# q projected from the raw activations, its mean taken out by a one-row matmul

## What is computed

```
x = x + 0.5 * ffn(layernorm(x))
x = x + attn(layernorm(x))
x = x + 0.5 * ffn(layernorm(x))

ffn(y):  xk = mu_k*y + (1-mu_k)*y_prev ; xr = mu_r*y + (1-mu_r)*y_prev
         sigmoid(xr @ Wr.T) * (square(relu(xk @ Wk.T)) @ Wv.T)
attn(y): q, k, v = y @ Wq.T, y @ Wk.T, y @ Wv.T ; a = sigmoid(y @ Wg.T)   (16 heads of 64)
         h_t = a_t * h_(t-1) + k_t v_t^T ; out_t = q_t^T h_t
         layernorm(out) @ Wo.T
```

## Time and profile before

| | |
|---|---|
| median of 2 runs | 5537.23 us (5469.79 and 5604.68) |
| profiled execution | 5486.97 us |
| its span, slowest core (core 0) | 5485.4 us |
| spans of the eight cores | 5455.2 to 5485.4 us |
| mean granted TensorE clock, core 0 | 0.750 |
| TensorE matmul busy | 4035.2 us, 74% |
| DVE busy | 2755.5 us, 50% |
| ACT busy | 1614.2 us, 29% |
| POOL busy | 705.8 us, 13% |

### The profile page before, as it was taken

How to read it: one execution, slowest core, us unless ns; L and a number is a source line. 1 busy time by engine, 2 the same in 40 slices (tenths; PEclk the granted TensorE clock), 3 DMA queues, 4 the chain that set the end, 5 groups by cost and what they waited for, 6 DMA issues and landing times.

```text
span 5485.4 us, 74827 instructions; the slowest of 8 cores (5455.2 to 5485.4 us)
## 1 busy us (share of the span) xinstructions
PE 4035.2 (74%) x20865; PEld 1801.9 (33%) x20865; DVE 2755.5 (50%) x7396; ACT 1614.2 (29%) x3334; POOL 705.8 (13%) x656
## 2 busy tenths in 40 slices
PE   5768677687776777767776777867778677686787
PEld 2423333233332333323333233332423324233242
DVE  4454454644546445464554645546455463554634
ACT  2224132232322323233231332313223132241322
POOL 1010110101101011110111101111020110201101
PEclk9678686886868768687786877858778586785866
DMA  9101000010000100001001010110100101010000
GB/s 162 47 16 50 21 31 24 16 51 20 31 24 16 52 19 32 23 16 53 18 33 33 5 53 18 33 38 1 54 17 33 38 24 31 16 49 22 16 24 16
DMA packets 125652, 174.88 MB, mean 32 GB/s; under 512 B 83912, under 2 KB 84176, under 8 KB 121040
## 3 DMA queue, kind: packets, MB, share of 16 engines
q10 hardware_dynamic: 13120, 83.89, 4.2%
q1 hardware_dynamic: 99392, 52.64, 3.6%
q0 software_dynamic: 12752, 33.56, 2.9%
HBM read 132.27 MB, written 37.75 MB: 31 GB/s over the span
## 4 chain that ended last, share of the span: by engine, by line
PE 59%; DVE 17%; issue 15%; ACT 6%; DVEq 1%; POOL 1%; DMA 0%; ACTq 0%; POOLq 0%
PE PA L126 22%; PE P L126 20%; PE PY L126 17%; DVE s_lams L722 3%; DVE s_dscr L514 2%; DVE s_scE L539 2%; DVE s_dscr L528 1%; DVE s_dscr L520 1%; ACT s_eps L729 1%; DVE s_VT L796 1%; ACT s_dscr L552 1%; DVE s_xb L689 1%; DVE s_scE L685 1%; DVE s_eps L733 1%; DVEq L102 1%
## 5 line engine op out<-in xcount | busy, mean ns | idle before, releaser
L722 DVE TENSOR_TENSOR_SCAN s_lams<-s_sgscr,s_zeros 128x64 f32<-128x64 f32 x1024 | 200.5, 269 | 512.2 <-ACT s_sgscr L716 509.2
L535 POOL TENSOR_TENSOR s_scE<-s_xb,s_lnb 128x512 bf16<-128x512 bf16 x256 | 296.3, 1189 | 1007.0 <-ACT s_lnb L454 935.5
L425 POOL TENSOR_TENSOR s_VT<-s_scE 128x512 bf16<-128x512 bf16 x112 | 116.1, 1037 | 2384.4 <-PE PA L126 2049.3
L929 DVE TENSOR_TENSOR s_htmp<-s_hst,PA 128x128 bf16<-128x128 bf16 x384 | 110.7, 288 | 535.4 <-PE PA L126 510.0
L126 PE MATMUL PA<-s_scB,s_W_wkf 128*128 128x512 bf16 x768 | 231.5, 437 | 179.5 <-DVE s_scB L544 170.3
L946 ACT CAST s_scE<-PY 128x128 bf16<-128x128 f32 x352 | 93.3, 265 | 787.5 <-PE PY L126 419.9
L126 PE MATMUL P<-s_scB,s_W_wkf 128*128 128x512 bf16 x768 | 219.4, 418 | 127.3 <-DVE s_scB L544 109.9
L126 PE MATMUL PA<-s_scA,s_scB 64*64 64x64 bf16 x1536 | 196.1, 241 | 147.0 <-DVE s_VT L796 76.3
L126 PE MATMUL PY<-s_scA,s_hst 64*64 64x64 bf16 x1408 | 199.4, 234 | 105.6 <-PE PY L126 14.3
L940 DVE TENSOR_SCALAR s_hst<-s_htmp,s_acs 128x64 bf16<-128x64 bf16 x1024 | 242.1, 280 | 58.6 <-DVE s_htmp L929 5.6
L126 PE MATMUL PY<-s_stS,s_VT 64*64 64x64 bf16 x1408 | 183.7, 244 | 110.0 <-DVE s_stS L858 56.9
(11 more groups left out here) (173 smaller groups left out, 7691.5 us busy)
## 6 DMA issues: line engine op xcount, KB each, us to landing
s_W_wg<-wo_s ACTq DMA_DIRECT2D x16, 2048.0 KB, 7.9
s_W_wg<-wg_s ACTq DMA_DIRECT2D x15, 2048.0 KB, 7.7
s_x_res<-x SPq DMA_DIRECT2D x16, 1024.0 KB, 7.7
s_x<-x SPq DMA_DIRECT2D x16, 1024.0 KB, 7.6
s_ktT<-s_scB SPq DMA_TRANSPOSE x512, 2.2
o<-s_x_res ACTq DMA_DIRECT2D x8, 1024.0 KB, 4.6
o<-s_x_res POOLq DMA_DIRECT2D x8, 1024.0 KB, 6.6
o<-s_x ACTq DMA_DIRECT2D x7, 1024.0 KB, 4.6
```

The source lines that it names most:

```text
L425: lambda e, j=j, sq_ap=sq_ap, src_t=src_t: e.tensor_tensor(sq_ap, src_t[:, TW * j:TW * j + TW], src_t[:, TW * j:TW * j + TW], ALU.mult),
L535: lambda e, j=j, u_ap=u_ap: e.tensor_tensor(u_ap, xb[:, TW * j:TW * j + TW], lnb[:, 0:512], ALU.add),
L722: e.tensor_tensor_scan(lam_ap[:, CH * cb:CH * cb + CH], loga_ap[:, CH * cb:CH * cb + CH], zeros64[:], 0.0, ALU.add, ALU.add),
L929: lambda e, j=j, bp=bp, PAu=PAu, ht_ap=ht_ap: e.tensor_tensor(ht_ap, hst[:, 64 * (4 * j + 2 * bp): 64 * (4 * j + 2 * bp) + 128], PAu[:, 12 ...
```

## The change

Wq is loaded first. Its row sums are made too (`fwsumq`), and the copies, the transpose and the trip through DRAM carry the sums of both Wo and Wq; they now stand behind the weights' loads. In the attention part q is projected from `xb`, the shadow of x as it is, and `wq_nm_step` adds the row sum of Wq times minus the mean to each tile. L689 now writes its result to `scE`, in place, and k, g and v are projected from there. Of the norms, the other stages and the rest of the order nothing is changed.

```diff
-    d_ws = nc.dram_tensor("ws", [NJ * 128], F32, kind="Internal").ap()
+    d_ws = nc.dram_tensor("ws", [2 * NJ * 128], F32, kind="Internal").ap()
...
-        wsumb = alloc("wsumb", [1, 1024], BF16)
+        wsumb = alloc("wsumb", [1, 2048], BF16)
...
         s.op("tensor", fwsum, reads=[("W", "wg"), ("onesb1",)], writes=[("P2",)])
-        s.op("scalar", lambda e: e.copy(lams[:, 40:48], P2[0:128, 40:48]),
-             reads=[("P2",)], writes=[("ws_s",)])
...
-        s.dma("gpsimd",
-              lambda e: e.dma_start(out=wsumb[:],
-                                    in_=d_ws.rearrange("(o c) -> o c", o=1)),
-              reads=[("ws_d",)], writes=[("wsum",)])
         s.dma("scalar_q",
               lambda e: e.dma_start(out=d_wo_s, in_=sb["W_wo"][:]),
               reads=[("W", "wg")])
-        for n in ["wkf", "wvf", "wr", "wq", "wk", "wv"]:
+        for n in ["wq", "wkf", "wvf", "wr", "wk", "wv"]:
...
+        def fwsumq(e):
+            for m in range(NJ):
+                for k in range(NJ):
+                    inst = MM(e, P2[0:128, 48 + m:49 + m],
+                              sb["W_wq"][:, D * k + 128 * m: D * k + 128 * m + 128],
+                              onesb1[:],
+                              start=(k == 0), stop=(k == NJ - 1))
+            return inst
+        s.op("tensor", fwsumq, reads=[("W", "wq"), ("onesb1",)], writes=[("P2",)])
+        s.op("scalar", lambda e: e.copy(lams[:, 40:56], P2[0:128, 40:56]),
+             reads=[("P2",)], writes=[("ws_s",)])
...
+        s.dma("gpsimd",
+              lambda e: e.dma_start(out=wsumb[:],
+                                    in_=d_ws.rearrange("(o c) -> o c", o=1)),
+              reads=[("ws_d",)], writes=[("wsum",)])
         s.dma("gpsimd",
               lambda e: e.dma_start(
                   out=sb["W_wg"].rearrange("p (i e) -> p i e", i=NJ),
...
                 s.op("vector",
                      lambda e, j=j, u_ap=u_ap: e.tensor_tensor(
-                         xb[:, TW * j:TW * j + TW], u_ap, lnb[:, 512:1024], ALU.mult),
-                     reads=[("uu", j), ("lnb_rs",)], writes=[("xb", j)])
+                         u_ap, u_ap, lnb[:, 512:1024], ALU.mult),
+                     reads=[("uu", j), ("lnb_rs",)], writes=[("u", j), ("uu", j)])
...
-            proj("wq", "u", scE, evac_q, chase=True, mid=emit_rs2, mid_at=1)
+            def wq_nm_step(e, P, m):
+                return MM(e, P[:, 0:TW], wsumb[0:1, 1024 + 128 * m:1024 + 128 * m + 128],
+                          ems[0:1, 0:512], start=False, stop=True)
+            proj("wq", "xb", xb, evac_q, chase=True, mid=emit_rs2, mid_at=1,
+                 extra_k=wq_nm_step, extra_reads=[("wsum",), ("em", 0)])
...
-            proj("wk", "xb", xb, evac_kk)
+            proj("wk", "u", scE, evac_kk)
...
-                                  xb[:, TW * k: TW * k + TW],
+                                  scE[:, TW * k: TW * k + TW],
...
-                            xb[:, TW * k + 256 * c + 128 * bp:
+                            scE[:, TW * k + 256 * c + 128 * bp:
```

More of the change, by code:

```diff
@@ L285, in build_program @@
                   writes=[("W", n)])
+        def fwsumq(e):
[9 more added lines that the diff above has]
+             reads=[("P2",)], writes=[("ws_s",)])
+        s.op("tensor",
+             lambda e: e.transpose(PA[2][0:16, 0:128], lams[:, 40:56], idf[:]),
+             reads=[("ws_s",), ("idf",)], writes=[("PA2",)])
+        s.op("scalar", lambda e: e.copy(lams[0:16, 128:256], PA[2][0:16, 0:128]),
+             reads=[("PA2",)], writes=[("ws_t",)])
+        s.dma("scalar_q",
+              lambda e: e.dma_start(out=d_ws.rearrange("(m d) -> m d", d=128),
+                                    in_=lams[0:16, 128:256]),
+              reads=[("ws_t",)], writes=[("ws_d",)])
+        s.dma("gpsimd",
+              lambda e: e.dma_start(out=wsumb[:],
+                                    in_=d_ws.rearrange("(o c) -> o c", o=1)),
+              reads=[("ws_d",)], writes=[("wsum",)])
         s.dma("gpsimd",
@@ L772, in g_mtile @@
                 s.op("tensor", fn,
-                     reads=[("W", "wg")] + [("xb", k) for k in range(NJ)],
+                     reads=[("W", "wg")] + [("u", k) for k in range(NJ)],
                      writes=[(Pk,)])
@@ L792, in vt_fill @@
                 s.op("tensor", fvt,
-                     reads=[("W", "wv")] + [("xb", k) for k in range(NJ)],
+                     reads=[("W", "wv")] + [("u", k) for k in range(NJ)],
                      writes=[(Pk,)])
```

## The result

The changed kernel is slower: 5523.22 us in the median against 5473.14 for the kernel before, a ratio of 1.0098 with a 95% interval of 1.0077 to 1.0118. That is some 50 us more, 3 a group: clear of the noise, but under the 2% that count as a change here.

A forecast was written before the change was run, and what follows sets the result against it. TensorE's path was taken to bound the kernel, over 16 groups. The profiled execution's 5487.0 us plus 16 for the groups (1.0 each) and 5 for the start gave 5508 us, range 5475 to 5575.

The forecast's parts named there:

- What the change removes, and the chase: q's first tile: the idle 2.5 us goes, matmuls stay 0.734 us apart, m=1 starts 2.66 us sooner.
- The price of a one-row matmul: q's tiles m=1 to 7: the extra matmul adds 0.41 us at the upper clock, 0.6 at the lower.
- the rule that I set against it: Skill page: 512 columns take 518 cycles whatever the rows; a group would cost about 1.2 us less, about break-even.
- The clock: In q, return 12.7 us after fb1 makes k 1.2 us later, return at 10.4 0.1 later; 1.0 a group taken.
- The wo row: Output projection, built like q: clock back 12.7 us after fb1, with m=1 at 7.34; used as the model for q.
- The start: Loading and summing Wq first delays the first group's shadows by 4.7 us; +5 taken, ends 0 and +14.
- a further weight takes 12 us: Weight loads at the start: Wq lands 12 us after Wo's 23.1, near 35 us.
- POOL's work behind the load of Wg is harmless: At the start, POOL's first other work comes after the queued loads (44.84 us before) and would have ws in time.
- Costed at nothing: k, g and v reading scE, written by L689: no cost, as DVE finishes about 14 us before k needs it.
- break-even: Rival: earlier clock return in most groups or one-row matmuls at 0.216 us; break-even or small gain, 5455 to 5490 us; chance 0.20.
- The granted clock of 0.81: Rival: dense stretches granted 0.81 from early on, 9.3 us a group; 5638 us, or past 5573; chance 0.12.
- The rival that I gave 0.03: q: idle time and slow chase both go, m=0 streams at 0.43, k 2.4 us sooner a group; 5454 us; chance 0.03.

The follow-up runs named there:

- e4_rows128: The changed kernel with q's extra matmul made of 128 rows, all but row 0 of its weights zero; ratio 1.0005, undisturbed die 5457 us.
- e3_rs_late: The changed kernel with the second norm's rstd broadcast recorded after q's tile m=6 instead of m=1; ratio 1.0066, undisturbed die 5492 us.
- e11_wos_late: The kernel before with only the start's edits, and the write of scaled Wo moved behind the sums' write; undisturbed die 5475 us.
- e2_late_sums: The changed kernel with the first loads in nearly the old order and Wq summed in the first group, before wr; ratio 1.0077, undisturbed die 5497 us.
- e5_no_chase: The changed kernel with chase=False for q, so m=0's eight matmuls and the extra are one operation; ratio 0.9988, undisturbed die 5422 us.

## Why the prediction was right and wrong

Its sum was 21 us over the profiled execution (16 for the groups, 5 for the start). Measured are 50: 30 to 32 for the groups and 19.5 for the start. The time, 5523, lies in the range, but the loss is more than double the one forecast, and against the median shown then, 5537, the forecast even read as a gain. That the time came within 15 us of the 5508 is part luck: the sum started from 5487, 14 above the median measured later, 5473.

**What the change removes, and the chase.** Right. q follows fb1 at once; the chase steps at 0.74 (forecast 0.734); m=1 starts 6.91 after fb1 (forecast 6.78).

**The price of a one-row matmul.** Right at both clocks: 2.15 us a tile at the upper level (833.96 - 831.81; forecast 2.14) and 3.99 at the lower (831.81 - 827.82; forecast 4.06). Of the rule that I set against it, that columns alone count (the Trainium skill, "TensorE: Matmul & The Clock Gate", Back-to-back issue gap), e4_rows128 says that it holds for matmuls of 128 rows (0.21 us) and not for one-row ones between them (0.41).

**The clock.** This is the step that failed in the groups. I took the return at 12.7 us after fb1 from wo and leaned to earlier. It was 15.2 in the third group. The whole miss of that group is there: of m=2 I had 0.32 at the lower clock, and it ran there in full, 0.68 x (3.99 - 2.15) = 1.25 us, and 24.9 + 1.25 = 26.15 is what was measured (the 24.9 was worked out from rows of the second group). What I overlooked stands in the earlier trace rows: in wo the rstd broadcast is recorded *ahead* of m=1, next to m=0's extra, where TensorE is half idle anyhow. In q it comes *behind* m=1, next to m=1's extra, in the middle of the first dense stretch. I used wo as a model of q and did not compare the order of the one-row matmuls. e3_rs_late shows that this one place is worth 15 us, about what the groups lost beyond the forecast.

The wo row was not a bad sample: over 16 groups of all eight cores of the kernel before, wo has the clock back 10.0 to 13.4 us after fb1. q in the changed kernel has it back 14.0 after fb1 in the mean (14.8 after the copy), and in e3_rs_late 11.7. The working of the sum held too: with 14.0 for 12.7 it gives k at 25.5 after fb1, and the mean over all cores is 25.6. Two things stay open. No run put the broadcast in q where wo has it; e3_rs_late only took it away. And in wo the clock has been down for some 90 us by then, while in q it falls about a microsecond before the copy.

**The start.** The direction and the mechanism were right, the term was mis-sized: 5 for 19.5, above even the end that I kept (14). The step that failed is "a further weight takes 12 us": Wq took 24. Twelve is the pace of the later weights, behind that write. Beside the write of Wo, wkf took 22 us from its issue in the earlier trace rows; I had this as a bound and should have taken it as the value, since Wq meets that write and the rest of x as well. e11_wos_late shows 9 to 11 us of it; the rest stays open. That POOL's work behind the load of Wg is harmless was right for the changed kernel (its first tile starts at 61.33, 0.16 us after the copy that it needs), and wrong only for e2_late_sums and e11_wos_late, where it cost what the earlier Wq had won.

**Costed at nothing (L689, scE for xb).** Right: the eight pairs are done soon after m=1 starts, and from k to g it takes 13.8 us before and after.

**The rivals.** Not break-even: the one-row matmul cost what wo showed. The granted clock of 0.81 did not appear at all; all cores of the profiled execution have 0.50 and 1.00 only. The rival that I gave 0.03, that the removed wait is worth what it looks like, is what e5_no_chase does with one more word in the code, and it ends faster than before.

## What to carry to other kernels

When a stage is priced by a sister stage, lay the two orders side by side, instruction by instruction: one small matmul in another place changed the clock's mean return by 2.4 us over all cores (14.8 against 12.4, e3_rs_late). In a stretch where the clock is to come back, keep TensorE on full matmuls without waits between them. Drop a chase (one operation and one wait for each accumulation step) as soon as its inputs are ready at its start; and pad a rank-one correction to 128 rows with zeros, if SBUF has the room. Before a transfer is put first, look at what else is on the DMA engines in those microseconds, and at what stands behind each wait on the issuing queue.

## What the runs showed of the hardware

- A one-row matmul of 512 columns between full ones takes 0.41 us at the upper clock, one of 128 rows 0.21. In the one-row form the tile's end and the next start are each about 0.1 us late.
- With full matmuls back to back the clock came back 3.4 us after the first (e5_no_chase); with the same eight 0.74 apart and one-row matmuls behind them, 14.7 us after the first (changed kernel, third group: 816.93 to 831.6). The moment at which it fell counts as well: that group of core 0 had it back at 10.4 after the copy, of core 1 at 16.0. Whether it is the rows, the time lost between matmuls, or both, that hold the clock down in the one-row form is not separated: e4_rows128 changes both.
- A weight of 2 MB in bf16 that is cast by its DMA lands some 12 us after the one before it where no write of that size runs beside it (wkf to wvf), and 24 us after it beside 1 to 2 MB of fp32 activations and a 2 MB write (changed kernel, Wo to Wq).
